# Hot rows weighed first, one one-hot per stretch, half of the keys normalised by GpSimd, edges prepared in four groups, weights issued by two engines

## The reference, cut to what matters

```python
xn = layernorm(x)
x  = x + gnn(xn, edge_weight, src, dst) + mix(xn)
x  = x + ffn(layernorm(x))               # mixture of 8 experts, capacity 489
# gnn: spmm(row, col, val, v) = segment_sum(val[:, None] * v[col], row)
h  = spmm(src, dst, edge_weight, xn)
z0 = softmax(spmm(..., h) @ W0.T + b0);  z1 = softmax(spmm(..., [z0, z0]) @ W1.T + b1)
gnn = tanh(concat(z0, z1) + h)
# mix: linear attention with 4 heads of 64
q, k, v = xn @ wq.T, layernorm_head(xn @ wk.T), layernorm_head(xn @ wv.T)
mix = (q @ (k^T v / S)) @ wo.T + bo
```

## Time and profile before

| | us |
|---|---|
| three executions | 1255.93, 1256.75, 1260.55 |
| the profiled execution | 1261.69 |
| its span (first to last instruction) | 1259.9 |

### The profile page before, as it was taken

One profiled execution on the slowest core, in us unless ns is written; L12 is line 12 of the kernel. 1 busy time (PEld: TensorE's weight loads), 2 busy tenths in 40 slices (PEclk: granted clock), 3 DMA queues, 4 the chain that ended last, 5 costly groups with the idle time before them and its releaser, 6 DMA issues.

```text
span 1259.9 us, 14147 instructions
## 1 busy us (share of the span) xinstructions
PE 1135.4 (90%) x4909; PEld 720.6 (57%) x4909; DVE 717.7 (57%) x1650; ACT 307.1 (24%) x1012; POOL 160.4 (13%) x203
## 2 busy tenths in 40 slices
PE   3678888887999999999997999999999669999995
PEld 2345555565666666666666444455557536666664
DVE  7997886988777777777772011113455504444433
ACT  2544544441122222222121111111112122222220
POOL 1123322340000000000000000000224421111111
PEclk8888888989999999999998999999999779999998
DMA  6101101111233433342224898787895363333420
GB/s 163 13 6 42 43 1 43 42 43 42 84 132 124 155 133 118 118 159 84 85 115 182 320 352 307 268 309 279 280 315 194 141 205 107 107 121 111 146 74 7
DMA packets 65862, 175.40 MB, mean 139 GB/s; under 512 B 16607, under 2 KB 49146, under 8 KB 53758
## 3 DMA queue, kind: packets, MB, share of 16 engines
q1 hardware_dynamic: 53230, 123.12, 28.6%
q10 hardware_dynamic: 8240, 43.30, 8.5%
q0 software_dynamic: 4320, 8.04, 1.8%
HBM read 113.82 MB, written 63.01 MB: 140 GB/s over the span
## 4 chain that ended last, share of the span: by engine, by line
PE 79%; DVE 9%; ACT 6%; issue 3%; ACTq 1%; another core or an unknown queue 1%; DMA 1%; POOL 0%; POOLq 0%; DVEq 0%
PE ps L1411 20%; PE ps L1558 19%; PE ps L1394 11%; PE ps L1664 9%; PE ps L1653 9%; PE ps L1378 2%; ACT W L670 2%; PE ps L1317 2%; PE ps L1436 2%; ACT RING L682 2%; PE ps L1385 1%; PE ps L1413 1%; PE ps L1594 1%; ACTq L637 1%
## 5 line engine op out<-in xcount | busy, mean ns | idle before, releaser
L1411 PE MATMUL ps<-RING,XX 128*128 128x512 f32 x600 | 294.7, 615 | 4.6 <-DVE W L993 4.4
L1558 PE MATMUL ps<-RING,RY 128*128 128x512 f32 (+2 forms) x750 | 281.0, 533 | 6.6 <-issue 6.6
L1394 PEld LDWEIGHTS ps<-RING 128*128 128x128 f32 x1250 | 166.5, 196 | 83.0 <-issue 80.6
L1558 PEld LDWEIGHTS ps<-RING,RY 128*128 128x128 f32 x750 | 137.3, 198 | 133.3 <-issue 131.1
L1394 PE MATMUL ps<-RING 128*128 128x128 f32 x1250 | 175.2, 282 | 36.3 <-ACT RING L682 34.1
L692 ACT COPY RING<-ps 128x512 f32<-128x512 f32 (+1 forms) x157 | 91.6, 584 | 348.0 <-PE ps L1394 330.8
L1411 PEld LDWEIGHTS ps<-RING,XX 128*128 128x128 f32 x600 | 108.5, 201 | 83.1 <-issue 83.0
L977 DVE TENSOR_TENSOR RING<-iota_n,RY 128x512 f32<-128x512 f32 (+1 forms) x157 | 108.4, 691 | 67.3 <-PE ps L1394 63.2
L983 DVE TENSOR_TENSOR RING<-iota_n,RY 128x512 f32<-128x512 f32 (+1 forms) x157 | 108.9, 694 | 0.0
L595 POOL DMA_INDIRECT xbuf_dram<-XX,sidx x25 | 25.4, 1015 | 643.4 <-DVE sidx L1240 637.9
L986 DVE TENSOR_TENSOR RING<-RING,RY 128x512 f32<-128x512 f32 x132 | 89.9, 681 | 0.0
(11 more groups left out here) (246 smaller groups left out, 1258.9 us busy)
## 6 DMA issues: line engine op xcount, KB each, us to landing
RING<-adj_dram SPq DMA_DIRECT2D x62, 1280.0 KB, 6.5
adj_dram<-RING ACTq DMA_DIRECT2D x31, 1280.0 KB, 4.6
XT<-in_L_ffn_w SPq DMA_DIRECT2D x8, 1024.0 KB, 7.8
RING<-in_L_ffn_w SPq DMA_DIRECT2D x8, 1024.0 KB, 6.7
rbuf_dram<-W SPq DMA_DIRECT2D x8, 516.0 KB, 5.1
RING<-rbuf_dram SPq DMA_DIRECT2D x8, 516.0 KB, 3.7
xbuf_dram<-W SPq DMA_DIRECT2D x8, 512.0 KB, 3.2
RING<-xbuf_dram SPq DMA_DIRECT2D x8, 512.0 KB, 4.7
```

Of the source, the lines that this page charges most:

```text
L1394: last = nc.tensor.matmul(o[:, i * P:(i + 1) * P], h[:, 0, i, :], h[:, 1, i, :], start=True, stop=(j != s))
L1411: last = nc.tensor.matmul(ps[:, ACC + dd, :], w, at, start=(j == 0), stop=True, skip_group_check=True)
L1558: last = nc.tensor.matmul(o, (Y if l == 0 else S0)[:, j, :], RING[:, slot_of[g % 5], i * across + first:i * across + first + w], start=(j ...
```

## The change

What it does, part by part:

1. ScalarE's `weigh(it-3)` moves ahead of `normal` and `squares(it)` in its iteration.
2. `spread` makes one one-hot instead of two (L923 goes); the payload L938 and `slots` L1364 read the one in the layout (stretch, column), so the moving operand of the 18 small matmuls is read with a step of 18 bf16 elements instead of 2.
3. The keys (256 of the 512 columns of `normed`) are normalised by GpSimd in its iteration `it`, after L570 and ahead of L575. `kvprod` waits for this too, through `s_kh`.
4. The edges are prepared in 4 groups instead of 6 (2, 4, 10 and 9 tiles).
5. The layer norm has two groups for variance and scale (7 and 18 tiles) instead of four; `stats` come at iterations 0, 1 and 2. At the start `prepare(0)` stands ahead of `scales(0)`. A first Sqrt on a constant loads ScalarE's table early.
6. Five weights are issued by SyncE after the windows of group 0 (and ahead of all of x but the first seven tiles) instead of ScalarE. One iota of GpSimd and one cast of VectorE go.

The diff, cut to its core:

```diff
-GROUPS = ((0, 2), (2, 6), (6, 11), (11, 16), (16, 21), (21, 25))
+GROUPS = ((0, 2), (2, 6), (6, 16), (16, 25))
-XG = ((0, 6), (6, 13), (13, 19), (19, 25))
-STATS_AT = {0: 1, 2: 2, 4: 3}
+XG = ((0, 7), (7, 13), (13, 19), (19, 25))
+LG = ((0, 7), (7, 25))
@@ SyncE
+                if g == 0:
+                    for to, src in ((wo_n, half("L0_mix_wo")), (wq_n, half("L0_mix_wq")), (W0_n, a["L0_gnn_W0"]),
+                                    (W1_n, a["L0_gnn_W1"]), (b1_n, a["L0_ffn_b1"])):
+                        sp.dma_start(to, src).then_inc(s_w, 16)
-                for x in {0: (1,), 1: (2, 3)}.get(g, ()):
+                for x in {0: (1, 2, 3)}.get(g, ()):
@@ GpSimd
+                if KV_LAG <= it < NT + KV_LAG:
+                    m = it - KV_LAG
+                    g, i = m // KT, m % KT
+                    gp.wait_ge(s_hscale, g + 1)
+                    ge(gp, s_kvt, m - 1)
+                    gp.tensor_tensor(khat[m % 2][:, 0:2, 0:P]..., KC[m % 6][:, 0:D]..., hrs[:, g % 2, i * NH:i * NH + 4]..., ALU.mult).then_inc(s_kh, 1)
                 if it > KV_LAG:
                     m = it - KV_LAG - 1
                     gp.wait_ge(s_khat, m + 1)
@@ ScalarE
+            act.wait_ge(s_const, 2)
+            nc.scalar.activation(rsum[:, 0, 0:1], ones_f[:, 0:1], ACT.Sqrt)
@@
                 if it < NT:
                     turned(it)
-                    if it + 3 < NT:
-                        normal(it + 3)
+                u = it - BUILD_IT
+                if 0 <= u < LEAD:
+                    weigh(u)
+                if it + 3 < NT:
+                    normal(it + 3)
...
                 if it < NT:
                     squares(it)
-                u = it - BUILD_IT
-                if 0 <= u < LEAD:
-                    weigh(u)
+                if it == 2:
+                    roots(1)
                 if 1 <= it <= NT:
                     kept(it - 1)
@@ VectorE
-                v.tensor_tensor(ohp[b].rearrange("p (c s i) -> p c s i", s=NR, i=2), ...
-                                g.rearrange("p (c i) -> p c i", i=2).unsqueeze(2).to_broadcast([P, C2, NR, 2]), ALU.is_equal)
@@
-                v.tensor_tensor(V[:, b, :].rearrange("p (c f s i) -> p c f s i", f=5, s=NR, i=2), ...
+                v.tensor_tensor(V[:, b, :].rearrange("p (f s c) -> p f s c", f=5, c=WC),
+                                ohs[b].rearrange("p (s c) -> p s c", c=WC).unsqueeze(1).to_broadcast([P, 5, NR, WC]),
+                                pay[:, :, j * WC:(j + 1) * WC].unsqueeze(2).to_broadcast([P, 5, NR, WC]),
                                 ALU.mult).then_inc(s_pay, 1)
@@ (head_scale)
-                link(v.reciprocal(r, r))
+                v.reciprocal(r, r).then_inc(s_hscale, 1)
+                dve.wait_ge(s_hscale, g + 1)
@@ (normed: groups 2:4, columns D:2 * D, only)
@@ (start)
             stats(0)
+            variances(0)
+            prepare(0)
             scales(0)
-            prepare(0)
             spread(0)
@@ (loop)
-                if it - 1 in STATS_AT:
-                    scales(STATS_AT[it - 1])
-                if it in STATS_AT:
-                    stats(STATS_AT[it])
+                if it == 3:
+                    scales(1)
+                if it < 3:
+                    stats(it + 1)
+                if it == 2:
+                    variances(1)
@@ TensorE
-                    last = nc.tensor.matmul(ps[:, MISC, 0:5 * NR], k[:, c // 2, :, c % 2], p[:, c // 2, :, :, c % 2], ...
+                    last = nc.tensor.matmul(ps[:, MISC, 0:5 * NR], k[:, c // 2, :, c % 2], p[:, :, :, c], ...
@@ (kvprod)
                 pe.wait_ge(s_khat, m + 1)
+                pe.wait_ge(s_kh, m + 1)
```

More of the change, by code:

```diff
@@ L143, in graph_program @@
         val_w = hb[:, 900:1350]
-        srcf, dstf, quo, diag, inv = (hb[:, 1350 + 90 * i:1440 + 90 * i] for i in range(5))
+        srcf, dstf, inv, quo, diag = (hb[:, i:i + 180] for i in (1350, 1530, 4806, 4986, 5166))
         grp = hb[:, 1800:2025].bitcast(BF16)
-        pay = hb[:, 2025:3150].bitcast(BF16).rearrange("p (c f i) -> p c f i", f=5, i=2)
+        pay = hb[:, 2025:3150].bitcast(BF16).rearrange("p (f n) -> p f n", f=5)
         rank = hb[:, 3150:3375].bitcast(F16)
@@ L342, in graph_program @@
         s_khat = sem("s_khat")
+        s_kh = sem("s_kh")
+        s_hscale = sem("s_hscale")
         s_kvt = sem("s_kvt")
@@ L416, in _ @@
             flat = lambda name: a[name].rearrange("(p t) -> p t", t=ET)
+            half = lambda name: a[name].rearrange("(r p) n -> p r n", p=P)
             sp.dma_start(dflat, flat("dst")).then_inc(s_dst, 16)
@@ L497, in _ @@
                         sp.wait_ge(s_khat, NT)
+                        sp.wait_ge(s_kh, NT)
                     elif g == 1:
@@ L628, in _ @@
             act.dma_start(X1[:, 0:XG[0][1], :], a["x"][0:XG[0][1] * P, :].rearrange("(j p) d -> p j d", p=P)).then_inc(s_x[0], 16)
-            for to, src in ((wo_n, half("L0_mix_wo")), (wq_n, half("L0_mix_wq")),
-                            (W0_n, a["L0_gnn_W0"]), (W1_n, a["L0_gnn_W1"]), (b1_n, a["L0_ffn_b1"]), (gate_w[:, :, :], half("L0_ffn_gate_w")),
-                            (bo_b[:, :], a["L0_mix_bo"].partition_broadcast(P)), (gb1_b[:, :], a["L0_gnn_b1"].partition_broadcast(P)),
+            for to, src in ((gate_w[:, :, :], half("L0_ffn_gate_w")), (bo_b[:, :], a["L0_mix_bo"].partition_broadcast(P)), (gb1_b[:, :], a["L0_gnn_b1"].partition_broadcast(P)),
                             (gate_b[:, :], a["L0_ffn_gate_b"].partition_broadcast(P)),
@@ L650, in roots @@
             def roots(g):
-                t = slice(*XG[g])
+                t = slice(*LG[g])
                 act.wait_ge(s_var, g + 1)
@@ L655, in normal @@
             def normal(j):
-                act.wait_ge(s_rstd, [j < t1 for _, t1 in XG].index(True) + 1)
+                act.wait_ge(s_rstd, 1 if j < LG[0][1] else 2)
                 nc.scalar.activation(XN[:, j, :], X1[:, j, :], ACT.Identity, bias=lnb[:, j:j + 1], scale=lnr[:, j:j + 1]).then_inc(s_xn, 1)
@@ L666, in squares @@
                 ge(act, s_khat, m - 5)
+                ge(act, s_kh, m - 5)
                 nc.scalar.copy(KC[m % 6], ps[:, PROD, :])
@@ L1028, in kv_tail, with stats, variances @@
                 v.engine_nop().then_inc(s_kvp, 1)
-            def stats(g):
-                dve.wait_ge(s_x[g], 16 if XG[g][1] < NT else 32)
-                for j in range(*XG[g]):
+            def stats(x):
+                dve.wait_ge(s_x[x], 16 if XG[x][1] < NT else 32)
+                for j in range(*XG[x]):
                     v.bn_stats(bst[:, j, :], X1[:, j, :]).then_inc(s_stats, 1)
-                dve.wait_ge(s_stats, XG[g][1])
-                variance(slice(*XG[g]))
+            def variances(g):
+                dve.wait_ge(s_stats, LG[g][1])
+                variance(slice(*LG[g]))
             def scales(g):
-                t = slice(*XG[g])
+                t = slice(*LG[g])
                 rstd(t, g + 1)
@@ L1317, in flip @@
                 return nc.tensor.transpose(dst, src, ident[0:n, 0:n])
-            pe.wait_ge(s_const, 10)
+            pe.wait_ge(s_const, 9)
             pe.wait_ge(s_cnt0, 1)
@@ L1363, in slots @@
                 for c in range(WC):
-                    last = nc.tensor.matmul(ps[:, MISC, 0:5 * NR], k[:, c // 2, :, c % 2], p[:, c // 2, :, :, c % 2], start=(c == 0), stop=(c == WC - 1))
+                    last = nc.tensor.matmul(ps[:, MISC, 0:5 * NR], k[:, c // 2, :, c % 2], p[:, :, :, c], start=(c == 0), stop=(c == WC - 1))
                 last.then_inc(s_slotted, 1)
```

43 lines of the change are left out of this document (16 added, 27 removed).

## The result

The changed kernel takes 1312.79 us, the median of four executions (1272.0 was the top of the range); the kernel before, in turn with it on the same chip, took 1258.65. The ratio is 1.043, with a 95% interval from 1.040 to 1.046: slower by 4.3%.

What follows compares the result with a forecast made beforehand. No engine fills stage B (products 7 to 24), bound by a chain; VectorE bounds stage A (16 to 89.57 us). -4.8 (A) +4.6 (B) +1 (C, 259 to 305) gives 1262.5 profiled, 1257.5 median; range 1238 to 1272, 8 in 10.

Steps and rivals of the forecast that it cites:

- so nothing is charged: Stage B, slots read with a step of 36 bytes: 0.6 us of cover, cost 0; at half speed 0.5 a turn.
- The tell-tale: Slot matmuls: if L1364 takes over 1.5 us at full clock in the profile after, the step of the read costs.
- The move of `weigh`: Stage B (product 7 to product 24): 1.30 us leaves the chain, short turn 8.80 to 7.5 if nothing else were late.
- The chain through GpSimd: Stage B: product, squares, kept, four GpSimd operations, `kvprod`, apply; turn 9.4 at full clock, bounds 8.4 to 10.3.
- Rivals 1 and 2: Stage B: 1, clock falls go, turn 9.4, 1243, 20 in 100; 2, GpSimd not late, turn 8.4, 1226, 12 in 100.
- the mean turn, 10.24: Stage B: turns of 9.4 and 11.1 alternate, about half each; +0.27 on 9.97, times 17: +4.6 us.
- stage A, -4.8: From 16 to 89.57 us, VectorE the bound: savings less added work sum to -4.8 us (-8 to -1).
- -2.4, -0.3 and +0.5: Stage A terms: L923 dropped -2.4, half of one `normed` -0.3, keys of tiles 0 and 1 on GpSimd +0.5.
- Rival 3: Stage B, `kvprod`'s wait: GpSimd's keys idle TensorE, a clock fall every turn; turn 11.1, +14.6, 1272; 20 in 100.
- The rule of the Trainium skill: VectorE and GpSimd exclude each other where VectorE is the bound: +2.3 us beyond the sum, 1260; 8 in 100.
- Rival 4: Stage A: `prepare` and x come later than thought because of SyncE; stage A gains 0, 1262; 5 in 100.
- the +1 of the forecast: Stage C, 259 to 305 us: GpSimd holds VectorE's L935 and L938; +1 us (-1 to +3).

Runs made afterwards that it cites:

- the pairs: Changed kernel with the second one-hot back, payload and slot matmuls reading it in pairs of columns (step of 4 bytes): 1269.93 us, ratio 1.0148.
- parts 1 and 3: Kernel before with only `weigh` moved ahead and half of the keys on GpSimd: 1266.17 us, ratio 1.0134.
- part 1 by itself: Kernel before with only `weigh` moved ahead of `normal` and `squares`: 1226.07 us, ratio 0.9787.
- parts 2 and 3 undone: Changed kernel with the second one-hot and paired slot reads back, and all keys on VectorE: 1210.72 us, ratio 0.9683.
- the single one-hot alone: Kernel before with only one one-hot, its slot matmuls reading with a step of 36 bytes: 1261.72 us, ratio 1.0087.
- part 3 undone: Changed kernel with all keys back on VectorE, the slot read with a step of 36 bytes kept: 1274.65 us, ratio 1.0115.
- groups of three: Kernel before with groups of 3 columns in place of pairs, a step of 6 bytes: 1259.73 us, one execution.

## Why the prediction was wrong

**The step that failed: "so nothing is charged" for the slots read with a step of 36 bytes.** I bounded it by cover (0.6 us) and by the clock, and set the size of the read itself to nothing, from the sentence that 1.3 us is already near the engine's pace. That argues for what the old read costs, not the new one; there was no row for the new one, and I gave it no upper bound. It measures 4.2 against 1.1 us on the chain. The tell-tale stood there (over 1.5 us at full clock), and the chain shows what it does: the slots now end 4.83 after the product (0.59 of ranks and 4.24), 2.57 later than the squares, and GpSimd's four operations start behind `kept`. 17 x 2.57 would be 44 us in stage B; its profiles differ by 21.5 there (206.16 against 184.69 with the pairs), for two reasons. A plain turn grows by 1.7 (9.6 to 11.26) and not by 2.57, because `kept` comes so late that GpSimd's four operations no longer lie beside VectorE's payload: from the start of `kept` to the end of the keys it is 3.07 us with the pairs and 2.15 here. And the turns of 11.0 to 11.3 with a fall in them grow only to 11.2 to 11.8. Another 8.1 are in stage A, where product 7 starts at 97.40 by the timeline (0.16 before the cut above), and at 89.30 with the pairs. In the whole kernel the ratios give 35 us.

**The move of `weigh`: right, and undervalued.** 1.30 us leaves the chain, but with the wait some falls of the clock went too (0.93 instead of 0.88): alone it brings 27 us, by the profiles all in stage B (142.6 instead of 169.6), where 7.5 a turn without falls would be 17 x 2.47 = 42 and was not a case that I priced. With GpSimd's chain in its place it can't show.

**The chain through GpSimd: right, in place and in size.** 9.6 for 9.4, the keys' end 5.33 for 5.45, the idle before `kvprod` as said: in the kernel with part 2 undone (product 7 to product 24), six of the 17 turns take 9.5 to 9.7 and six 11.0 to 11.3, taking turns, as forecast. Rivals 1 and 2 fall: the clock stays at 0.89 there, and only one turn of 17 (8.6) is below 9. The point that this makes the kernel slower is shown by two pairs of runs: 0.9683 to 1.0148 with the keys moved to GpSimd (58 us), and back to 0.9721 when the same operation stands first.

**Term mis-sized: the mean turn, 10.24.** It measures 184.69 / 17 = 10.86 in that kernel. The twelve plain turns have a mean of 10.35; the other five (12.5, 11.8, 8.6, 15.2, 12.4) stand around `prepare` and `head_scale` and have a mean of 12.1, which is 8.7 us that the sum left out. In the one of 15.2, VectorE's payload starts at 186.90, behind `prepare`, 4 us after the product's start; slots and `kept` follow at 188.33 and 190.50, and the keys beside VectorE's next operations take 1.73. The keys on GpSimd are not what makes this turn long: it takes 15.5 with the keys on VectorE, and 11.1 with the keys on GpSimd but the old groups (parts 1 and 3). Its `prepare` has 162 columns and takes 5.2 us instead of 3.2; the sum had nothing in stage B for the larger groups, neither for this turn nor for the two turns that lose their `prepare`.

**Term mis-sized: stage A, -4.8.** With the keys on VectorE and pairs, product 7 starts at 85.68 against 89.41 before (timeline), -3.7. The terms of the sum that are in that kernel (all but -2.4, -0.3 and +0.5) make -2.6, and part 1 by itself has -0.7 (88.72), for which I charged nothing here: the terms on VectorE were right (`prepare` has 16 instructions and not 17, which changes nothing). But with the keys on GpSimd it starts at 89.30. The chain at its end:

```profile
79.38 2.15 PE ps L1386 x18
81.55 0.28 ACT RY L691
...
83.42 1.70 POOL W L583
...
85.26 1.20 PE ps L1408 x4
86.46 3.01 PE ps L1434 x4
```

The keys of tile 1 take 1.70 instead of 0.58, and `kvprod` and apply behind them run at half clock. I charged +0.5; it is 3.6. The rest, 97.40 against 89.30, is the read with the step: TensorE is busy 71.7 of 81.6 us, and is nearly the bound where VectorE was.

**The rivals.** Rival 3 named the right mechanism (the keys keep TensorE idle, "the strided slots would help it"), but priced the slots at 0.5 and so ended at 1272. The rule of the Trainium skill (page "SBUF — State Buffer", section "Who interferes with whom") that I weighed at 2.3 us is seen in L587's 2.64 us beside L944's 2.74; but with the keys first in GpSimd's iteration the kernel's time shows next to nothing of it. Rival 1's 1243 is not the 1238 from which the range starts; the sum gives no reason for these 5 us. Rival 4 is close to what stage A did, for another reason: the x tiles and windows came in time enough, since 85.68 was reached with SyncE's order as changed.

**How it adds up.** By ratios, from the kernel with parts 2 and 3 undone (0.9683): keys on GpSimd +58 us, the read with a step on top of that +35, together 1.043. Taken in the other order, the read is +54 and the keys +40: each hides part of the other, since both lengthen the same turn. The +6.2 behind product 24, against the 1 forecast, can be parted at the last matmul of `kvprod` in the traces, which starts at 284.5 before and at 336.7 after. From product 24 to there it is 25.4 us before and 33.0 after, +7.6; what follows takes 975.4 and 974.0. With the pairs this piece is 26.5 us, so the +1 of the forecast was right for the chain that it had, and the rest is the read with the step once more.

## What to carry to other kernels

Before a layout is changed to save an instruction on one engine, price the read of it on every engine that reads it, and give a read that has no row an upper bound as well. An operation moved to a free engine is placed in that engine's order, and inherits every wait ahead of it: here the same operation costs 54 us more behind the wait for `kept` than ahead of it. When an engine's order ties several others together, add the turns in which one of them is late (`prepare`, `head_scale`) apart from the plain ones.

## What the runs showed of the hardware

A bf16 matmul of 130 columns pays for the step between the elements of its moving operand: 18 of them take 33.1 / 25 = 1.3 us at 4 bytes, 1.8 at 6, 3.3 at 12, 4.5 at 18 and 4.4 at 36, in the mean of the 25 tiles. Between neighbours that is about 0.06 us at 4 bytes (1.09 / 18, the chain above) and 0.24 at 36 (4.24 / 18). Single matmuls, ns min/median/max, before and after:

```profile
L1364 PE MATMUL ps<-W,RY x450: 218/221/313, 34.5 to 270.2; 128*128 128x130 bf16 x150
```

```profile
L1377 PE MATMUL ps<-W,RY x450: 392/413/418, 31.5 to 321.3; 128*128 128x130 bf16 x150
```

With the large step the granted clock doesn't show in their time. At 4 bytes the 18 take 1.25 us at full clock and 2.13 at half (at 43.48 in the kernel before). At 36 bytes they take 4.36 to 4.39 in all 25 tiles of the changed kernel, of the one with the single one-hot alone and of the one with part 3 undone, also in the 4.39 us from 43.08 in the kernel with part 3 undone, where the mean granted clock is 0.57. So what sets their pace there is the read and not the array's clock, and a fall that lies in them costs nothing by them.

VectorE's payload of 2340 bf16 elements takes 1.4 us at its shortest when input and output have one layout, in pairs or with the stretch layout; 1.9 in groups of three, and 2.45 in the mean when it reads one layout and writes the other.

TensorE's clock also fell where the engine had no idle in its rows (the ends of matmuls are modelled in them). In the kernel with the single one-hot alone it is busy 173.0 of 173.0 us from 97 to 270, at a mean granted clock of 0.93. Busy time by stretch around one fall:

```profile
121.00:122.00 1.00, 1.00 (x6) 0.52 (x5) 0.96 (x2) 0.83 (x3) 0.00 (x0) 0.92 0.00 0
122.00:123.00 1.00, 1.00 (x6) 0.58 (x4) 0.97 (x3) 0.00 (x0) 0.00 (x0) 0.50 0.00 0
```

It goes from 2.4 to 1.2 GHz inside the 18 slot matmuls with the step, which last from 118.84 to 123.21, and so do the other six falls of this stretch. In the kernel before, each of the 12 falls of stage B begins 0.1 to 1.5 us behind the idle of 1.9 us before `build`; here they come in the slow reads. Rows without idle are thus no sign that the clock stays up.
